# A Mamba-style scan in a two-layer block: the product with C of every other group of states on GpSimd instead of VectorE, with the order of all steps written anew

## What is computed

```python
dt = softplus(einsum('blr,cr->blc', dbl[..., :DT_RANK], W_dt) + b_dt)
Bs = dbl[..., DT_RANK:DT_RANK + D_STATE]
Cs = dbl[..., DT_RANK + D_STATE:]
def step(h, inp):
    dt_t, B_t, C_t, u_t = inp
    dA = exp(dt_t[:, :, None] * A)
    h = h * dA + (dt_t * u_t)[:, :, None] * B_t[:, None, :]
    y = einsum('bcs,bs->bc', h, C_t)
    return (h, y)
```

## Time and profile before

| what | value |
|---|---|
| median of 3 runs | 2882.52 us |
| lowest and highest run | 2879.82 and 2882.74 us |
| the profiled execution | 2874.39 us |
| its span on the core | 2872.6 us |
| TensorE, VectorE busy | 2416.6 us (84%), 2214.2 us (77%) |
| ScalarE, GpSimd busy | 1202.6 us (42%), 654.9 us (23%) |
| mean granted TensorE clock | 0.911 |

### The profile page before, as it was taken

One profiled execution on the slowest core, in us unless ns is written; L12 is line 12 of the kernel. 1 busy time (PEld: TensorE's weight loads), 2 busy tenths in 40 slices (PEclk: granted clock), 3 DMA queues, 4 the chain that ended last, 5 costly groups with the idle time before them and its releaser, 6 DMA issues.

```text
span 2872.6 us, 60547 instructions
## 1 busy us (share of the span) xinstructions
PE 2416.6 (84%) x22424; PEld 1916.6 (67%) x22424; DVE 2214.2 (77%) x5056; ACT 1202.6 (42%) x2697; POOL 654.9 (23%) x465
## 2 busy tenths in 40 slices
...
GB/s 129 4 1 3 7 4 1 8 3 8 3 7 2 3 8 3 7 4 1 8 3 8 3 7 2 3 8 3 7 4 1 8 3 8 3 7 2 1 6 2
DMA packets 24830, 21.39 MB, mean 7 GB/s; under 512 B 7217, under 2 KB 21570, under 8 KB 24530
## 3 DMA queue, kind: packets, MB, share of 16 engines
...
## 4 chain that ended last, share of the span: by engine, by line
issue 40%; PE 30%; DVE 19%; POOL 6%; ACT 1%; POOLq 0%; DVEq 0%; ACTq 0%
PE banks L1001 7%; PE banks L1027 4%; PE banks L875 3%; PE banks L993 3%; DVE wide L1370 2%; DVE wide L1358 2%; POOL lg L553 2%; DVE inv L1544 2%; PE banks L1019 2%; PE banks L852 2%; POOL rq L525 2%; DVE inv L1540 1%; PE banks L983 1%; PE banks L1049 1%; PE banks L1041 1%
## 5 line engine op out<-in xcount | busy, mean ns | idle before, releaser
L549 POOL TENSOR_TENSOR wide<-wide 128x512 f32<-128x512 f32 x128 | 264.7, 2068 | 778.9 <-DVE wide L1378 429.1
L1493 DVE SCALAR_TENSOR_TENSOR wide<-pad,conv,wide 128x256 f32<-128x256 f32 x864 | 370.0, 496 | 0.0
L1370 DVE TENSOR_TENSOR_SCAN wide<-wide 128x1024 f32<-128x1024 f32 x128 | 292.9, 2289 | 1.9 <-ACT wide L655 0.3
L1164 PE MATMUL banks<-inv,up 128*128 128x256 f32 x1024 | 266.2, 389 | 0.0
L1174 PE MATMUL banks<-down,inv 128*128 128x128 f32 x2048 | 262.7, 277 | 0.0
L1174 PEld LDWEIGHTS banks<-down,inv 128*128 128x128 f32 x2048 | 252.3, 192 | 5.7
L655 ACT ACTIVATE wide<-small,a_neg 128x255 f32<-128x255 f32 x512 | 216.0, 497 | 90.0 <-DVE wide L1370 80.6
L783 ACT ACTIVATE inv<-banks,up1b 128x256 f32<-128x256 f32 x512 | 213.2, 483 | 89.7 <-PE banks L1164 88.8
L736 ACT COPY inv<-banks 128x512 f32<-128x512 f32 x160 | 92.7, 579 | 345.4 <-DVE inv L1540 271.1
L1001 PE MATMUL banks<-inv,mats 64*64 64x64 f32 x5120 | 186.1, 234 | 52.9 <-DVE inv L1540 34.5
L1001 PEld LDWEIGHTS banks<-inv,mats 64*64 64x64 f32 x5120 | 176.0, 148 | 71.1 <-issue 69.7
...
## 6 DMA issues: line engine op xcount, KB each, us to landing
...
```

Of the source, the lines that this page charges most:

```text
L549: g.tensor_tensor(ypart[p % 2], r[:, 0:512], r[:, 512:1024], ALU.add).then_inc(a_yp.h, 1)
L1164: last = t.matmul(bank(3 + half, T, q * T), up1[:, e, m * P:(m + 1) * P], xxT, start=True, stop=True)
L1370: v.tensor_tensor_scan(state[st % 2], decay[st % 2], drive[st % 2], 0.0, ALU.mult, ALU.add).then_inc(a_h.h, 1)
L1493: v.scalar_tensor_tensor(dst, src, w, dst, ALU.mult, ALU.add).then_inc(c_conv.h, 1)
```

## The change

For odd `st` the product with C moves from VectorE to GpSimd. ScalarE copies the spread of C from bank 1 into a new SBUF tile `c_kept` (128x512); GpSimd waits for the scan and for the copy, multiplies in place, and then adds the pair. For even `st` nothing changes. TensorE's next spread of C waits for the copy instead of the product. The semaphores `a_rp` and `a_Cs` are new; the three of the triangular solve (`c_tp`, `c_lp`, `c_X`) become one handle, `c_slv`, and the two of the attention's projections become one. `keep_warm` takes its count from a table `WARM` by step, in place of the constant 2; the steps not in it get 0. All four strings in `TURNS` are new.

```diff
 def a_scan(i, st):                      # GpSimd
     if 1 <= st <= NG:
         p = st - 1
-        g.wait_ge(a_rd.h, a_rd.at(i, p + 1))
+        if p % 2 == 0:
+            g.wait_ge(a_rd.h, a_rd.at(i, p // 2 + 1))
+        else:
+            g.wait_ge(a_h.h, a_h.at(i, p + 1))
+            g.wait_ge(a_Cs.h, a_Cs.at(i, p // 2 + 1))
+            r4 = state[p % 2].rearrange("p (q c t) -> p q c t", q=SG, c=CB)
+            g.tensor_tensor(r4, c_kept[:].rearrange("p (q t) -> p q t", t=T).unsqueeze(2).broadcast_to([P, SG, CB, T]), r4,
+                            ALU.mult).then_inc(a_rp.h, 1)
+            g.wait_ge(a_rp.h, a_rp.at(i, p // 2 + 1))
         if p >= 2:
             g.wait_ge(a_yq.h, a_yq.at(i, p - 1))
...
+def a_read(i, st):                      # ScalarE
+    if st < NG and st % 2 == 1:
+        if st >= 3:
+            s.wait_ge(a_rp.h, a_rp.at(i, st // 2))
+        s.wait_ge(a_C.h, a_C.at(i, st + 1))
+        s.copy(c_kept[:], bank(1)).then_inc(a_Cs.h, 1)
...
 def a_read(i, st):                      # TensorE
     if st + 1 < NG:
-        t.wait_ge(a_rd.h, a_rd.at(i, st + 1))
+        if st % 2 == 0:
+            t.wait_ge(a_rd.h, a_rd.at(i, st // 2 + 1))
+        else:
+            t.wait_ge(a_Cs.h, a_Cs.at(i, st // 2 + 1))
         spread(NS + (st + 1) * SG, 1).then_inc(a_C.h, 1)
...
 def a_read(i, st):                      # VectorE
-    if st < NG:
+    if st < NG and st % 2 == 0:
...
 "gpsimd": (
-    "yyxyyyyyyxxxxxxxxxxxyyxyxxx"),
+    "yyyyxyyxyyxxxxxxxxyxxyxyxxx"),
...
-            def keep_warm(bk):
+            def keep_warm(bk, *step):
-                for _ in range(FILL):
+                for _ in range(WARM.get(step, 0)):
```

More of the change, by code:

```diff
@@ L129 @@
     "tensor": (
[L130 to L131 removed]
+        "yyyyyyyyxyxyyyxxyyyyyyxyyyxyxyyxyxyyxxyxyyyyyxyyxxyyxxyxxyxxyxxyxyxxxyyxxxxyxxyyxxyyyxyyyxyxyxyx"
+        "yyyxyyyyyxyyxyyxyyxyyxyyyxyxyyxyxxyyyyyxyx"),
     "vector": (
[L133 to L134 removed]
+        "xyyyyxyyxxyxyyyyyxyyxyyyxyxyxyyxyxyyxyxyyxyxyyyxyxyxxyxxyxyxxxyxxxyxxyxxyxxyxxyxyxxxyxyyxxxyyyxy"
+        "xxxxxyxyxxyxyxxyxxxyyyy"),
     "scalar": (
[L136 removed]
+        "yyyxxyxxyxxyxyxyxxxyyyxxxyyxyyyxxxxyxxxxxyxxxyxxxyxxyyyyxxyyxxxyyxyyxyyxyxxyyxxyyxyxyxyxxyxyxx"),
     "gpsimd": (
[L138 removed]
+        "yyyyxyyxyyxxxxxxxxyxxyxyxxx"),
+}
+WARM = {
+    ("c_top", 1): 2, ("c_low", 0): 2, ("c_X", 0): 2, ("c_low", 1): 2, ("c_X", 1): 2, ("c_O", 0): 2, ("c_O", 1): 2,
+    ("c_S",): 2, ("c_kS",): 2, ("c_turn_o",): 2, ("c_out",): 2, ("d_turn",): 2, ("d_qkv",): 2, ("d_scores",): 2,
+    ("d_turn_p",): 2, ("d_av",): 2, ("d_a",): 2, ("d_gates",): 2, ("d_turn_g",): 2, ("d_yinit",): 2,
 }
@@ L384, in build @@
         c_kS = sig("c_kS_ps"); c_R0, c_R1 = sigs("c_R", 1, 3)
[L385 to L386 removed]
+        c_slv = sig("c_solve_ps", 6); c_tx = sig("c_top", 2); c_low = sig("c_low", 2)
+        c_U = sig("c_U", 2); c_Uw = sig("c_Uw")
         c_Sp = sig("c_S_ps"); c_S = sig("c_S"); c_O = sig("c_O_ps", 2); c_O2 = sig("c_O2_ps")
@@ L786, in _ @@
             follow(s, TURNS["scalar"], dict(a_turn=lambda i: modulate(i, 0, 0), a_in=a_in, a_silu=a_silu, a_xproj=a_xproj, a_soft=a_soft,
-                           a_scan=a_scan, b_turn=lambda i: modulate(i, 1, 0), b_soft=lambda i: sp_exp(i, 0), b_up=b_up_,
+                           a_scan=a_scan, a_read=a_read, b_turn=lambda i: modulate(i, 1, 0), b_soft=lambda i: sp_exp(i, 0), b_up=b_up_,
                            c_turn=lambda i: modulate(i, 2, 0), c_beta=c_beta, c_soft=lambda i: sp_exp(i, 1), c_proj=c_proj,
@@ L877, in a_out_ @@
             def a_out_(i):
+                keep_warm(0, "a_out")
                 if isinstance(i, int):
@@ L888, in b_logits @@
             def b_logits(i):
+                keep_warm(1, "b_logits")
                 t.wait_ge(ln_h[1].h, ln_h[1].at(i, 1))
@@ L989, in c_prod @@
                 if n >= 2:
+                    keep_warm(7, "c_prod", gr, half)
                     t.wait_ge(c_AT.h, c_AT.at(i, n - 1))
@@ L1030, in c_top @@
             def c_top(i, ch):
-                if ch == 1:
-                    keep_warm(4)
+                keep_warm(7 if ch == 0 else 4, "c_top", ch)
                 if ch == 0:
@@ L1050, in c_low_ @@
                                     start=True, stop=True)
-                last.then_inc(c_lp.h, 1)
+                last.then_inc(c_slv.h, 1)
             def c_X_(i, ch):
-                keep_warm(7 - ch)
+                keep_warm(7 - ch, "c_X", ch)
                 t.wait_ge(c_low.h, c_low.at(i, ch + 1))
```

61 lines of the change are left out of this document (31 added, 30 removed).

## The result

| | before | after |
|---|---|---|
| median of 4 runs | 2882.63 us | 2932.99 us |
| lowest and highest | 2879.82, 2886.93 | 2927.45, 2942.32 |
| ratio on record, 95% | | 1.0196 [1.0165, 1.0227] |
| profiled execution, its span | 2874.39, 2872.6 | 2927.45, 2925.7 |
| mean granted TensorE clock | 0.911 | 0.911 |

The change makes the kernel about 2% slower; 2922 us was predicted. The two medians divided give 1.0175, which lies in the interval. Of the experiments, one execution of e5 (8619 us) and one of e9 (4553 us, the profiled one, so that e9 has no trace to read) were disturbed; they are left out of the ratios, and without them the medians would be 3012.45 and 2857.98 us.

The account below looks back on a forecast made before the run. VectorE was taken to bound the scan stage, TensorE the last 35.2 us of a pass. Scan end -0.3, tail +2.2, chain +1.3, slack -0.5 gave +2.7 us a pass, +40 over 15, first sample -1: 2922 us, range 2854 to 2960.

Parts of the forecast that it names:

- The -4.86: Scan stage: four products with C leave VectorE at 1.215 us each, 4.86 us less a pass.
- The +1.2: Scan stage: VectorE waits for TensorE at more places, 1.2 us a pass, between 0 and 3.95.
- The holds: Scan stage: scans wait for GpSimd's running instructions, 3.4 us a pass, bounds 0.4 and 9.2.
- The tail: Last scan's end to `a_y`: 6.3 us instead of 4.05, +2.2 a pass, bounds +1.2 and +3.5.
- The chain: Behind the scan: `c_O` ahead of `a_out` +0.5, `c_gated` before the softplus +1.4, `b_norm2` -0.6; sum +1.3 us.
- The slack of 0.5: Second half, where the samples' chains meet before TensorE's full stretch: some tenths of slack, 0.5 us taken off a pass.
- term of +1.4 for `c_gated`: Chain behind the scan: `c_gated` before the softplus starts GpSimd's root 1.4 us later, +1.4 a pass.
- The first sample: First sample's scan before the loop: some 1 us gained for each of three pairs, tail 2.2 lost; -1, 3 either way.
- VectorE's busy time: Sign in the changed profile: about 25 us lower, not 78, since held scans count as busy.
- Rival 1: Faster, 30%: scans held only by tenths (0.4 us), slack of 2 us ahead of the full stretch; -1.8 a pass, 2855.
- Rival 3: Much slower, 9%: GpSimd's product takes 3.6 us, adds come late for scans; +6.7 us a pass, 2982.
- Rival 4: Scan stage: TensorE idles more and gets less clock, some 1 us a pass on top, 2937; counted with the forecast, together 52%.

Follow-up runs that it names:

- e5: The change with TensorE's old order at the scan's end (last final-sum matmul before `c_X` 1, `a_out` before `c_O` 1), on TensorE only: 3012.88 us, 1.046.
- e9: e7 plus the first half's start in its old place, `a_res` and `b_norm` ahead of `c_o` 1, GpSimd's square behind its root: 2858.4 us, 0.9943.
- e3: The change with GpSimd's product cut to one column in 256, waits, copies and order kept: 2905.0 us, 1.0095.
- e1: The change's new order with all eight products on VectorE, no ScalarE copies: 2994.89 us, 1.0411.
- e2: The kernel before, in its old order, with the odd products moved to GpSimd and copies added on ScalarE: 2952.04 us, 1.026.
- e7: The change with group 7's product back on VectorE, TensorE's old tail order, `c_U` 1 behind `a_y`, `c_gated` behind the softplus: 2914.6 us, 1.0116.
- e4: The change with `c_gated` put back behind the softplus on VectorE, nothing else: 2905.74 us, 1.0102.
- e12: e11's order with all eight products on VectorE, read 3 put behind the solve's steps: 2860.77 us, 0.9942.
- e11: e9 with group 5's product also back on VectorE, so GpSimd keeps only groups 1 and 3: 2855.73 us, 0.9934.
- e6: The change with the start of the first half (`a_norm2` and what follows it) in its old place on all engines: 2903.91 us, 1.0092.

## Why the prediction was right

The forecast case held: slower, by a relief that does not come through, a longer tail, and a chain behind it. By its steps, per pass:

| step | predicted | measured |
|---|---|---|
| GpSimd's product | 2.3 us | 2.35 us |
| reads taken off VectorE before the last scan's end | -4.86 | -3.65 |
| holds by GpSimd | +3.4 | +2.2 |
| VectorE waiting for TensorE in the scan stage | +1.2 | +1.2 (all that remains) |
| last scan ends | -0.3 | -0.27 |
| the tail | +2.2 | +2.08 |
| chain up to `b_select` | +1.3 | +0.7 |
| from `b_select` to the full stretch | -0.5 | +0.8 |
| pass | +2.7 | +3.31 |
| first sample | -1 | +4.8 |

- **The -4.86 was wrong by one read.** The fourth of the odd reads, of group 7, stands behind the last scan: in the kernel before it is what releases the last add. It can't bring the last scan forward; 3 x 1.215 = 3.65 do. The sum -0.3 came out right because the holds were over-rated by as much: they are 1.6 us in scans and 0.6 in `c_R`'s product, in the mean of a pass.
- **The +1.2 is right by luck.** It was meant as waiting for TensorE. What remains is -2.37 us for the earlier start of scan 0, +2.8 for the four steps of the inversion that now stand in the stretch, and +0.9 of idle time, less 0.1 of overlap. Only the last of these was in the prediction.
- **The holds.** Scan 6 was forecast to lose 2.0 us; in the pass shown it loses 1.88. Its mean is 1.64. Scan 4's 0.9 us was right in size and wrong in place: the short SBUF step of `c_R`, one row ahead of scan 4, met the add first and took the 0.92, though only in ten of the 15 passes. Scans 1 and 2 lost 0.1 and nothing instead of 0.2 and 0.3. The rows that told beforehand were the 3.18 us add and the 1.498 us convolution step, and not the scan's own 2.386: that one had met the last tenths of an add.
- **The tail.** 6.3 us behind the scan was forecast, 6.13 measured. e3 shows that the reason given was only half of it: with a product of 0.2 us the gap is even longer, 6.93, for `c_X` 1 stands ahead in TensorE's order. Either of the two alone makes the tail long (7.04 us in e1 with no product on GpSimd, 6.50 in e2 with the old order), and e7 had to mend both.
- **The chain.** `c_O` ahead of `a_out` cost 0.3 us (0.5 forecast). `b_norm2` is free of GpSimd's square, as forecast (0.62 us for its two steps instead of 1.31), but the square now meets the second step of `a_res` instead, which takes 0.92 us and not 0.42 in every pass: 0.1 us is left of the 0.6. `b_select` follows `b_logits` after 7.53 us instead of 7.02: +0.5, not +1.4. The root on GpSimd starts 1.0 us later behind `b_logits`, since a part of `c_gated` fits into the wait for ScalarE; and it takes 2.90 us instead of 3.40, because `c_gated`, two steps with all operands in SBUF, no longer runs beside it:

```profile
1294.94 3.40 POOL L553 TENSOR_TENSOR lg<-sp,expo 128x16 f32<-128x16 f32 x1 [1.70 <-DVE sp L1298]
```

```profile
1320.78 2.90 POOL L568 TENSOR_TENSOR lg<-sp,expo 128x16 f32<-128x16 f32 x1 [4.79 <-DVE sp L1335]
```

- **The slack of 0.5 isn't there.** Every delay at `b_select` arrives in the full stretch, and 0.8 us come on top. They are `c_gated`'s too, by way of TensorE and its clock, as shown behind the tail above and undone by e4. The prediction's term of +1.4 for `c_gated` came near the 1.3 that it costs in all (0.5 and 0.8; e4 takes off 1.6 a pass), but by another path than the one it gave; that the sum came near is luck.
- **The first sample** was the worst single step: -1 forecast with 3 either way, +4.8 measured. I gave each pair of groups a gain and no hold, although the rule of the loop's scans applies there too: scans 2, 4 and 6 come behind a drive product with GpSimd at work, and lose 5.2 us together. The tail adds 1.9. e12 has 154.5 us for this stretch again, e11 with two products 156.5.
- **VectorE's busy time** fell by 37.5 us, where 25 was forecast and 78 would be the reads alone.

Rival 1 (2855 us) needed small holds and a slack: the 4.16 us scan and the pass's +3.31 speak against both. Rival 3 needed a product of 3.6 us: it never takes over 2.362. Rival 4 looked for a lower clock in the scan stage, where it rose (0.87 to 0.91); it fell behind `b_select`, and cost 0.8 us a pass there. In e1, e2 and e5 the mean of the execution fell too (0.893, 0.890 and 0.898), where TensorE waits more; the rows above price single places, and how much of their time is the clock's in all wasn't separated.

That the order was a cost of its own, beside the product, was not in the prediction as one term, only as pieces (`c_gated`, `c_X` and `c_O`, `a_norm2`). `a_norm2`'s move was named beside the 1.2 us of waiting and had no price of its own: e6 shows that it and what follows it cost 29 us, nearly 2 us a pass, because they stand at the head of the scan's chain. It was the largest term that was missing. That scan 0 still came 2.37 us earlier than before is by other moves of the new order, the four steps of the inversion above all.
